# 16-head windowed attention: ScalarE squares the projected queries behind the copies of the late probabilities, and copies the early outputs ahead of the second turned queries

## What is computed

```python
q = _rmsnorm(_rope(heads(x @ wq.T)), q_norm_w)      # 16 heads
k = _rmsnorm(_rope(x @ wk.T), k_norm_w)             # one head
scores = einsum('bqgtd,bqgsd->bqgts', q, k) / sqrt(64)
scores = where((cols <= rows) & (rows - cols <= 128), scores, -1e30)
attn = softmax(scores)
out = einsum('bqgts,bqgsd->bqgtd', attn, v)
return out @ wo.T
```

```python
def _rope(x):     # theta = t * freqs; even and odd channels are rotated against each other
    r1 = x1 * cos - x2 * sin
    r2 = x1 * sin + x2 * cos
def _rmsnorm(x, w):
    return x * rsqrt(mean(x * x) + EPS) * w
```

## Time and profile before

| what | value |
|---|---|
| median of 3 runs | 3207.71 us (3206.38 to 3210.78) |
| the profiled execution | 3208.76 us, its span 3207.0 us |
| busy over the span | PE 94%, DVE 67%, ACT 54%, POOL 37% |
| the main phase of this attention | 2225 to 2871 us of the span |
| rounds with a rotate behind them (n = 0 to 60) | squares first at 2228.1, last at 2825.0 us |
| mean granted clock of PE | 0.986 |

### The profile page before, as it was taken

The page is one execution under the profiler, slowest core; times in us unless marked ns, Lnnn a source line. Parts: engine busy times, 40 slices in busy tenths (PEclk is TensorE's granted clock), DMA queues, the critical chain, the costliest instruction groups (busy, mean ns, idle before and its releaser), DMA issues. The chain is left out here.

```text
span 3207.0 us, 61051 instructions
## 1 busy us (share of the span) xinstructions
PE 3012.3 (94%) x22529; PEld 1889.7 (59%) x22561; DVE 2147.3 (67%) x4191; ACT 1736.0 (54%) x3881; POOL 1170.7 (37%) x1151
## 2 busy tenths in 40 slices
PE   7999989999999999999899999997899999989999
PEld 6999867446565655467565543334566666664444
DVE  7999835106474645359669744447999999956777
ACT  1322334566667566657535443344666666665666
POOL 4666611001010101018357323225777777740000
PEclk9999989999999999999999999999999999999999
DMA  2000000000000000000000032210000000004776
GB/s 92 16 16 16 1 19 13 1 1 8 3 5 7 4 5 4 4 7 2 9 1 1 28 76 54 58 43 19 17 7 5 5 5 5 4 25 43 68 67 66
DMA packets 75679, 66.43 MB, mean 21 GB/s; under 512 B 20518, under 2 KB 70857, under 8 KB 74969
## 3 DMA queue, kind: packets, MB, share of 16 engines
q1 hardware_dynamic: 75384, 62.52, 11.6%
HBM read 55.58 MB, written 2.51 MB: 18 GB/s over the span
## 5 line engine op out<-in xcount | busy, mean ns | idle before, releaser
L743 ACT ACTIVATE p_hidden<-p_hid_ps,net_bias 128x344 f32<-128x344 f32 x816 | 382.4, 549 | 225.7 <-PE p_hid_ps L690 167.1
L716 PE MATMUL p_y_ps<-p_hidden,net_down 128*64 128x344 f32 x1632 | 286.0, 467 | 4.6 <-DVE p_hidden L792 4.6
L2875 DVE TENSOR_TENSOR p_hid<-p_silu,p_pair_ps 128x344 f32<-128x344 f32 x288 | 134.8, 509 | 161.5 <-PE p_pair_ps L2824 82.5
L690 PE MATMUL p_hid_ps<-xn,net_up 64*128 64x344 f32 x1248 | 238.0, 481 | 1.2 <-PEq L333 0.6
L792 DVE TENSOR_TENSOR p_hidden<-p_hidden,p_row 128x344 f32<-128x344 f32 x384 | 175.1, 514 | 78.8 <-ACT p_hidden L743 44.1
L2856 ACT ACTIVATE p_silu<-p_pair_ps 128x344 f32<-128x344 f32 x288 | 116.0, 454 | 190.8 <-PE p_pair_ps L2813 190.8
L1983 POOL TENSOR_TENSOR p_prob<-p_prob,p_total 128x1024 f32<-128x1024 f32 (+1 forms) x128 | 185.3, 1469 | 52.5 <-DVE p_total L2171 52.5
L2546 POOL TENSOR_TENSOR p_qt<-p_qt,p_q_sum 97x512 f32<-97x512 f32 (+1 forms) x44 | 46.4, 1054 | 427.3 <-DVE p_q_sum L2489 427.3
L716 PEld LDWEIGHTS p_y_ps<-p_hidden,net_down 128*64 128x64 f32 x1632 | 103.3, 136 | 160.6 <-issue 49.7
L1970 POOL TENSOR_TENSOR p_rot<-p_rot,p_cross 128x512 f32<-128x512 f32 x128 | 160.1, 1273 | 96.4 <-DVE p_cross L2145 96.4
L2802 POOL TENSOR_TENSOR p_weighted<-routed_hn,sent_row 128x344 f32<-128x344 f32 x96 | 89.1, 950 | 241.3 <-PE p_pair_ps L2829 206.3
(11 more groups left out here) (487 smaller groups left out, 8045.9 us busy)
## 6 DMA issues: line engine op xcount, KB each, us to landing
sent_row<-gated_rows SPq DMA_DIRECT2D x192, 86.0 KB, 2.9
p_row<-mark_rows SPq DMA_DIRECT2D x192, 86.0 KB, 10.3
tok_x<-in_tok_x SPq DMA_DIRECT2D x11, 384.0 KB, 3.1
out<-h SPq DMA_DIRECT2D x12, 172.0 KB, 3.6
shared_swapped<-xn SPq DMA_DIRECT2D x64, 32.0 KB, 1.9
shared_value_pairs<-shared_values SPq DMA_DIRECT2D x16, 128.0 KB, 2.5
p_x<-in_tok_x SPq DMA_DIRECT2D x5, 384.0 KB, 3.1
p_kinds<-in_tok_c3w SPq DMA_DIRECT2D x1, 1280.0 KB, 7.2
```

The source lines that it names most:

```text
L690: mm = pe.matmul(hid_ps[k % ring][:, 0:TILE], w_up[half(g), n, :], x[half(g), cols(t)], start=True, stop=not experts or by_rows)
L716: mm = pe.matmul(y_ps[u][half(g), 0:TILE], w_down[:, n, :], hid[k % hidden_ring][:], start=n == 0, stop=last and not experts)
L743: act.activation(hid[k % hidden_ring][:], hid_ps[k % ring][:, 0:TILE], func, bias=b_up[:, n:n + 1]).then_inc(act_done.sem, 1)
L2875: dve.tensor_tensor(hid[n % ring_h][g][:], silu[n % 2][g][:], c_of(n, g)[:, 0:TILE], ALU.mult).then_inc(hid_ready.sem, 1)
```

## The change

Only ACT's list in the rounds is put in another order. The instructions, their operands, their waits and all other engines' lists stay as they are. In each round the copy of the early outputs, copy_out(n - 2, EARLY), moves from behind copy_queries(n + 1, 1) to ahead of it, and squares(n + 3) moves from between the two copies of queries to behind the two copies of late probabilities, ahead of exponentials(n, LATE).

```diff
                 for n in range(BATCHES + 1):
                     if n + 1 < BATCHES:
                         copy_queries(n + 1, 0)
-                    if n + 3 < BATCHES:
-                        squares(n + 3)
+                    if n >= 2:
+                        copy_out(n - 2, EARLY)
                     if n + 1 < BATCHES:
                         copy_queries(n + 1, 1)
-                    if n >= 2:
-                        copy_out(n - 2, EARLY)
                     if n >= 4 and n % 2 == 0:
                         copy_output((n - 4) // 2)
                     if n >= 1:
                         copy_late(n - 1, 0)
                         copy_late(n - 1, 1)
+                    if n + 3 < BATCHES:
+                        squares(n + 3)
                     if n < BATCHES:
                         exponentials(n, LATE)
                     if n >= 1:
```

## The result

The changed kernel takes 3260.5 us (median of 4 runs, 3251.2 to 3264.5), beside 3208.4 for the kernel before. The ratio is 1.0155, with a 95% interval of 1.0142 to 1.0168: slower by 1.6%, where +1.2% was forecast, and 4.5 us over the range.

What follows compares the result with a forecast made beforehand. PE and DVE, 92 to 93% busy, were taken to bound the kernel; a closed loop would add 38.5 us over 60 rounds, less 0.4 at the end: 3207.7 + 38.1, say 3246 us, range 3239 to 3256.

Steps and rivals of the forecast that it cites:

- Step 2, the closed loop: Squares behind late copies make DVE's rotate hang on the round's own reciprocal: rounds of 10.29 us for 9.65, 38.5 us more.
- Step 3: On ACT, exponentials, early copy and late outputs start about 0.9 us later in each round; claimed hidden.
- the fit of the other engines: Other engines fit into 10.29 us rounds: PE by 0.13 us, POOL by 0.2, SP's loads with rounds of slack.
- PE's margin of 0.13 us in even rounds: PE's work in a round with an output adds up to 10.16 us, fitting into 10.29 by 0.13 us.
- Step 1, the early outputs: Early outputs copied ahead of second queries in odd rounds: at most 34.7 us of PE's waits, nothing where DVE sets pace.
- a rival of its own with 6%: PE's clock falls in odd rounds' new 2.0 us pauses, slowing 30 scores: 43 us more, 3289 us; chance 6%.
- a sign of being wrong: A granted clock of PE under 1.00 in the phase would show the forecast wrong.

Runs made afterwards that it cites:

- the kernel with fillers: Changed kernel with 7 products of ones (3 behind an end_round) on PE in the pause ahead of each odd round's late transposes: 3245.3 us, ratio 1.0123.

## Why the prediction was wrong, and where it was right

The sign and the mechanism of the loop held; the size was short by 14 us of 52. Of these, 10.35 are the slow rounds, 1.2 the loop (10.31 us for 10.29), and some 2.5 neither.

- **Step 2, the closed loop: right, and nearly to the number.** Each term stands in the trace as it was taken: the rotate at 5.07 us, DVE's idle time 1.16 us for 1.24 in a plain round, 10.31 us for 10.29. That is 39.7 us for 38.5. Doubling the squares shows the slope. That the kernel with fillers comes to 617.14 us for 617.4 is in part luck: 60 plain rounds are 618.6, and the fillers also shorten the odd rounds.
- **Step 3 and the fit of the other engines: right.** The exponentials, the roots and the copies behind them are hidden, POOL's addition fits, and the last rounds give back 0.4 us. PE's margin of 0.13 us in even rounds is there too; but it is what makes the clock dear, since a slow score has nothing to hide behind.
- **Step 1, the early outputs: right to count nothing here.** Alone they gain 5 us in 60 rounds; inside the loop nothing, as the kernel with the squares alone has the same ratio.
- **The failing step is the clock.** The sum has no term for PE's clock: it was put at nothing, and its fall was held to be a rival of its own with 6%, all 30 odd rounds at 43 us or none. What came lies between: four groups in the 30 odd rounds, two falls each, 2.5 us a group, 10 us in all, and a mean granted clock of 0.98 from 2300 to 2850 us, which the prediction had named as a sign of being wrong. The price of the first fall was well sized: PE loses 5.40 - 3.83 = 1.57 us, where 1.56 was written, less the margin of 0.13, and the round is 11.75 - 10.31 = 1.44 us longer, where 1.43 was written. But the loss is spread over the early transposes, mix_late and the score, and not the score's alone. The number of falls was wrong, and the second fall, into the transposes of the loop, was not foreseen. The ground for the low chance was a pause of 2.05 us in the trace before that was followed by the full rate. It was one draw: in the changed kernel the same pause ahead of the loop, with no edit near it, is followed by slower transposes (1.37 us for eight instead of 1.09), as its timeline has it:

```profile
2233.85 1.37 PE L1893 MATMUL p_t_ps<-ident,shared_end_scores 128*128 128x128 f32 x8 [2.06 <-POOL shared_end_scores L1993]
```

  The 10 us belonged into the forecast's own sum, or at least into the range, whose upper end of 3256 would then have been some 3266.
- **About 2.5 us are neither.** In the profiles 1.6 us lie ahead of the first reciprocal and behind the last, and the medians differ by 0.9 us more than the spans. A range around a single profiled execution has to carry that, and the 1 us of spread at its upper end was too little; without the 10 us of the clock, though, the median would have been 3250, inside the range.

The Trainium skill, "TensorE: Matmul & The Clock Gate", Part 4, says that transposes do not count as activity of PE the way matmuls do. The runs do not contradict it, and do not show it either: the clock fell where a pause of 2.0 us lies between transposes, and three plain products in the pause kept it up, but pauses of 1.12 us between the same transposes were followed by no fall. No run has plain products on both sides of such a pause, so the transposes' part is not separated from the pause's.

## What to carry to other kernels

An engine with a third of its time free can still set the pace: ask of every instruction in a hand-written order what its predecessors in the list wait for, and whether one of these waits leads back to the instruction itself in the same round. Here a move by a few places made an operation that hung on nothing but an early product hang on the round's own reciprocal, and the loop's length, added up from single rows, gave the new round to 0.02 us. And when a change opens regular pauses of about 2 us on TensorE, put some rounds at the lower clock into the sum; a few products into a bank that is overwritten anyway brought them back here, 0.3% in all.

## What was not expected of the hardware

The clock's falls are rare and regular at once. With a pause of 2.00 us in three of four odd rounds and of 1.12 us in the fourth, long rounds begin at 12, 24, 36 and 52 in one execution and at 20, 36, 46 and 60 in another of the same kernel. The groups have one shape: 1.44 us over a plain round, then about 0.6 to 0.8 and 0.3 to 0.5, at times with two plain rounds behind the first. Pauses cut to about 1.3 us set off none in the profile that was taken.
